# A state-space scan regrouped into turns over both channel halves of four sequences

## The reference

```
u = silu(conv(xin));  dt = softplus(...);  A = -exp(A_log)
def step(h, inp):                       # over 128 tokens
    dt_t, B_t, C_t, u_t = inp
    dA = exp(dt_t[..., None] * A)       # 256 channels x 16 states
    h = dA * h + (dt_t * u_t)[..., None] * B_t[:, None, :]
    y = einsum('bcn,bn->bc', h, C_t)    # sum over the 16 states
y = (y + u * D) * silu(z);  out = y @ wo.T
```

## Time and profile before

| | us |
|---|---|
| median of 3 runs | 2901.29 |
| profiled execution | 2900.32 |
| its span | 2898.6 |
| scan stage of layer 0, 1, 2 | 275.5, 259.5, 244.5 |
| DVE busy over the span | 1628.0 (56%) |
| PE busy | 2225.7 (77%) |
| POOL busy | 974.6 (34%) |

### The profile page before, as it was taken

The page is one execution under the profiler, slowest core; times in us unless marked ns, Lnnn a source line. Parts: engine busy times, 40 slices in busy tenths (PEclk is TensorE's granted clock), DMA queues, the critical chain, the costliest instruction groups (busy, mean ns, idle before and its releaser), DMA issues. The chain is left out here.

```text
span 2898.6 us, 39071 instructions
## 1 busy us (share of the span) xinstructions
PE 2225.7 (77%) x13654; PEld 1455.9 (50%) x13654; DVE 1628.0 (56%) x3279; ACT 1077.1 (37%) x2217; POOL 974.6 (34%) x926
## 2 busy tenths in 40 slices
PE   6999877999998668936539997569996388765691
PEld 4666544777787556934115555245553122244351
DVE  2333458656660141214259997689996799824352
ACT  2221112444443211412646663546663566401110
POOL 3001105445556013041015554045550366502104
PEclk7656567999999756977759999679998699956796
DMA  5000001111111003720000000000000000000462
GB/s 198 0 0 0 23 20 39 36 31 31 31 33 26 16 7 112 219 73 11 15 6 1 1 1 1 2 6 1 1 1 3 0 0 1 0 7 14 141 195 62
DMA packets 167830, 98.74 MB, mean 34 GB/s; under 512 B 89975, under 2 KB 151747, under 8 KB 166130
## 3 DMA queue, kind: packets, MB, share of 16 engines
q1 hardware_dynamic: 163058, 87.75, 10.9%
q0 software_dynamic: 4608, 8.86, 1.1%
HBM read 58.34 MB, written 38.80 MB: 34 GB/s over the span
## 5 line engine op out<-in xcount | busy, mean ns | idle before, releaser
L1255 POOL TENSOR_TENSOR mc_hc<-mc_states,mc_c_sb 128x1024 f32<-128x1024 f32 x192 | 452.8, 2358 | 327.6 <-DVE mc_states L1316 304.9
L1316 DVE TENSOR_TENSOR_SCAN mc_states<-psum,mc_dbu 128x1024 f32<-128x1024 f32 x192 | 439.8, 2290 | 14.6 <-issue 0.4
L1345 PE MATMUL psum<-mc_hc,ident 128*128 128x512 f32 x768 | 373.4, 609 | 6.5 <-POOL mc_hc L1255 6.5
L1277 ACT ACTIVATE mc_c_sb<-psum 128x512 f32<-128x512 f32 x384 | 225.7, 588 | 107.1 <-PE psum L1336 107.1
L1268 ACT ACTIVATE psum<-dt,a 128x1016 f32<-128x1016 f32 x192 | 213.5, 1112 | 110.9 <-DVE mc_states L1316 110.8
L1305 DVE TENSOR_TENSOR mc_dbu<-psum,dtu 128x1024 f32<-128x1024 f32 x192 | 233.5, 1216 | 9.9 <-PE psum L1328 9.0
L1345 PEld LDWEIGHTS psum<-mc_hc,ident 128*128 128x128 f32 x768 | 148.9, 195 | 126.5 <-issue 96.9
L594 POOL TENSOR_TENSOR fw_tmp<-zeros 128x30 f32<-128x30 f32 (+14 forms) x240 | 123.3, 514 | 256.4 <-DMA zeros<-fw_blocks 238.2
L1336 PE MATMUL psum<-bc,select 96*128 96x512 bf16 x384 | 152.6, 397 | 71.0 <-ACT mc_c_sb L1277 70.9
L1336 PEld LDWEIGHTS psum<-bc,select 96*128 96x128 bf16 x384 | 37.6, 98 | 272.1 <-ACT mc_c_sb L1277 254.2
L1670 POOL DMA_INDIRECT c_y<-slots_y,slots x64 | 64.0, 1000 | 306.0 <-PEq L1665 287.1
(11 more groups left out here) (379 smaller groups left out, 4455.8 us busy)
## 6 DMA issues: line engine op xcount, KB each, us to landing
e_w<-in_L_ffn_ew SPq DMA_DIRECT2D x64, 256.0 KB, 3.1
slots_x<-zeros SPq DMA_DIRECT2D x12, 1024.0 KB, 12.6
e_x<-slots_x SPq DMA_DIRECT2D x96, 128.0 KB, 2.3
slots_y<-e_y SPq DMA_DIRECT2D x96, 128.0 KB, 2.0
e_w<-in_L_ffn_w SPq DMA_DIRECT2D x64, 128.0 KB, 2.2
fw_blocks<-fw_A SPq DMA_DIRECT2D x128, 32.0 KB, 1.7
zeros<-fw_blocks SPq DMA_DIRECT2D x8, 512.0 KB, 3.4
fw_inverses<-fw_Y SPq DMA_DIRECT2D x8, 512.0 KB, 3.1
```

The source lines that it names most:

```text
L1255: nc.gpsimd.tensor_tensor(hc[:, k % 2, :], states[:, k % 2, :], c_sb[:, k % 2, :], ALU.mult).then_inc(s["hc_done"], 1)
L1277: nc.scalar.activation(c_sb[:, k % 2, j * 512:(j + 1) * 512], c_ps, ACT.Copy).then_inc(s["c_copied"], 1)
L1316: nc.vector.tensor_tensor_scan(out=states[:, k % 2, :], data0=decay_ps, data1=dbu[:, k % 2, :], initial=0.0, op0=ALU.mult, op1=ALU.add).th ...
L1345: last = nc.tensor.matmul(y_ps[:, j * 512:(j + 1) * 512], m.ident, hc[:, k % 2, j * 512:(j + 1) * 512], start=(n == 0), stop=(n == NSTATE ...
```

## The change

- A turn now covers both halves of four sequences (2 x 512 columns), so one B row and one C row serve both halves. There are still 64 turns per layer, in 4 chunks of 16, and two scans of 512 columns per turn.
- B: PE spreads the first `SPLIT` columns into `b_ps` (256 of 512 in layers 0 and 1, 320 in layer 2), which DVE multiplies for both halves. The other 256 (192) columns go to `rest_ps`, ACT copies them to `b_sb`, and POOL multiplies them two turns ahead (`rest`).
- C: the step-size stage copies the C rows to SBUF (ACT, four copies of 32x512) and writes them to DRAM; in the scan stage SP loads each row, broadcast to 128 partitions, up to four turns ahead.
- Accumulation: 8 matmuls of 32x32 weights (`eye`) per turn in place of 2 of 128x128. Half 1 goes from row group i to column group i+1; the weights of half 1 are permuted on the host to fit.
- u*D is 8 tile matmuls more at the start of each chunk (`skip_path`), and `finish` multiplies by the gate; the output stage loses its gating.
- LSTM: `whh` in two 64x64 quarters (8 matmuls for 4); the parts of the cell in one DVE instruction; the cell itself by two PE matmuls of 128x128 weights (`lstm_cell`), placed behind the accumulation of turn k-2 in PE's order.

The added lines of the scan, with what stands around them:

```diff
+    if f == 0:
+        for g in range(GROUPS):
+            act.wait_ge(s["split_done"], g + 1)
+            nc.scalar.activation(rows[DTR:2 * DTR, g, :], m.bank[g][DTR:2 * DTR, :], ACT.Copy).then_inc(s["rows_done"], 1)
...
+    CHUNKS = GROUPS
+    TURNS = CHUNKS * NSTATE
+    SPLIT = GT - (256 if lstm else 192)
...
+for k in range(TURNS):
+    c, cols, n = turn(k)
+    if k >= AHEAD:
+        sp.wait_ge(s["hc_done"], k - AHEAD + 1)
+    sp.dma_start(c_sb[:, k % AHEAD, :], c_rows[n:n + 1, cols].to_broadcast([P, GT])).then_inc(c_in[k % AHEAD], 16)
+    if k == NSTATE and layer < 2:
+        load_front(sp, io, m, z, layer + 1)
...
+def rest(k):
+    c, cols, n = turn(k)
+    pool.wait_ge(s["b_copied"], k + 1)
+    nc.gpsimd.tensor_tensor(dbu[:, k % 2, :, SPLIT:GT], z["dtu"][:, :, c * GT + SPLIT:(c + 1) * GT],
+                            b_sb[:, k % 2, :].unsqueeze(1).to_broadcast([P, HALVES, GT - SPLIT]), ALU.mult).then_inc(s["rest_done"], 1)
+rest(0)
+rest(1)
 for k in range(TURNS):
+    pool.wait_ge(s["scan_done"], 2 * k + 2)
+    pool.wait_ge(c_in[k % AHEAD], 16 * (k // AHEAD + 1))
     if k >= 2:
         pool.wait_ge(s["y_mm"], k - 1)
+    nc.gpsimd.tensor_tensor(hc[:, k % 2], states[:, k % 2], c_sb[:, k % AHEAD, :].unsqueeze(1).to_broadcast([P, HALVES, GT]),
+                            ALU.mult).then_inc(s["hc_done"], 1)
+    if k + 2 < TURNS:
+        rest(k + 2)
...
+def decay(k, f):
+    c, cols, n = turn(k)
+    if k >= 1:
+        act.wait_ge(s["scan_done"], 2 * (k - 1) + f + 1)
+    nc.scalar.activation(decay4[:, f, :, 1:P], z["dt"][:, f, cols].rearrange("p (b t) -> p b t", b=GS)[:, :, 1:P], ACT.Exp,
+                         scale=z["a"][:, f, n:n + 1]).then_inc(s["decay_done"], 1)
+def copy_b(k):
+    act.wait_ge(s["rest_mm"], k + 1)
+    if k >= 2:
+        act.wait_ge(s["rest_done"], k - 1)
+    nc.scalar.activation(b_sb[:, k % 2, :], rest_ps, ACT.Copy).then_inc(s["b_copied"], 1)
+nc.scalar.activation(decay4[:, :, :, 0:1].rearrange("p f b o -> p (f b) o"),
+                     z["dt"][:, 0, 0:HALVES * GS].unsqueeze(2), ACT.Copy, scale=0.0)
+if lstm:
+    nc.scalar.activation(cell_ps, r["cell"][:, :], ACT.Copy).then_inc(s["cell_set"], 1)
+copy_b(0)
+copy_b(1)
...
+    decay(k, 0)
     if lstm:
         act.wait_ge(s["step_mm"], k + 1)
+        nc.scalar.activation(gates[:, :], step_ps[:, 0:3 * BATCH], ACT.Tanh)
+        nc.scalar.activation(fresh_ps, step_ps[:, CELL * BATCH:(CELL + 1) * BATCH], ACT.Tanh).then_inc(s["gates_done"], 1)
+    decay(k, 1)
     if lstm:
+        act.wait_ge(s["cell_mm"], k + 1)
+        nc.scalar.activation(tanh_ps, cell_ps, ACT.Tanh, scale=0.5).then_inc(s["tanh_done"], 1)
+    if k + 2 < TURNS:
+        copy_b(k + 2)
...
+def finish(c):
+    dve.wait_ge(s["y_mm"], NSTATE * (c + 1))
+    cols = slice(c * GT, (c + 1) * GT)
+    nc.vector.tensor_tensor(z["y"][:, :, cols], y_ps, z["gate"][:, :, cols], ALU.mult).then_inc(s["y_done"], 1)
 for k in range(TURNS):
+    c, cols, n = turn(k)
+    dve.wait_ge(s["b_mm"], k + 1)
+    nc.vector.tensor_tensor(dbu[:, k % 2, :, 0:SPLIT], b_ps[k % 2][:, 0:SPLIT].unsqueeze(1).to_broadcast([P, HALVES, SPLIT]),
+                            z["dtu"][:, :, c * GT:c * GT + SPLIT], ALU.mult).then_inc(s["dbu_done"], 1)
+    if n == 2 and c > 0:
+        finish(c - 1)
     if lstm:
         dve.wait_ge(s["gates_done"], k + 1)
+        nc.vector.scalar_tensor_tensor(out=parts[:, :], in0=gates[:, BATCH:3 * BATCH], scalar=1.0, in1=fresh_cell_ps, op0=ALU.add,
+                                       op1=ALU.mult).then_inc(s["parts_done"], 1)
+    dve.wait_ge(s["dbu_done"], k + 1)
+    dve.wait_ge(s["rest_done"], k + 1)
     if k >= 2:
         dve.wait_ge(s["hc_done"], k - 1)
+    for f in range(HALVES):
+        dve.wait_ge(s["decay_done"], 2 * k + f + 1)
+        nc.vector.tensor_tensor_scan(out=states[:, k % 2, f, :], data0=decay_ps[:, f, :], data1=dbu[:, k % 2, f, :], initial=0.0,
+                                     op0=ALU.mult, op1=ALU.add).then_inc(s["scan_done"], 1)
+        if lstm and f == 0:
+            dve.wait_ge(s["tanh_done"], k + 1)
+            nc.vector.scalar_tensor_tensor(out=hs[:, first_step + k + 1, :], in0=gates[:, 0:BATCH], scalar=1.0, in1=tanh_ps,
+                                           op0=ALU.add, op1=ALU.mult).then_inc(s["hidden_done"], 1)
...
+def tiles(weights, src, f, start, stop):
+    for i in range(P // QUARTER):
+        rows = slice(QUARTER * i, QUARTER * (i + 1))
+        to = QUARTER * ((i + f) % (P // QUARTER))
+        last = nc.tensor.matmul(y_ps[to:to + QUARTER, f, :], weights[rows, :], src[rows, :], start=start, stop=stop,
+                                skip_group_check=True)
+    return last
+def skip_path(c):
+    if c > 0:
+        pe.wait_ge(s["y_done"], c)
+    else:
+        pe.wait_ge(s["diag_done"], 2)
+    for f in range(HALVES):
+        last = tiles(diag[:, f, :], z["u"][:, f, c * GT:(c + 1) * GT], f, True, False)
+    last.then_inc(s["du_mm"], 1)
 def accumulate(k):
+    c, cols, n = turn(k)
+    if n == 0:
+        skip_path(c)
     pe.wait_ge(s["hc_done"], k + 1)
+    for f in range(HALVES):
+        last = tiles(eye[:, :], hc[:, k % 2, f, :], f, False, n == NSTATE - 1)
     last.then_inc(s["y_mm"], 1)
...
+        for d in range(2):
+            rows = slice(HD * d, HD * (d + 1))
+            last = nc.tensor.matmul(step_ps[rows, q * BATCH:(q + 1) * BATCH], r["whh"][rows, q, rows], hs[rows, first_step + k, :],
+                                    start=False, stop=(q == GATES - 1), skip_group_check=True)
     last.then_inc(s["step_mm"], 1)
+def lstm_cell(k):
+    pe.wait_ge(s["parts_done"], k + 1)
+    nc.tensor.matmul(cell_ps, half_ident[:, :], parts[:, BATCH:2 * BATCH], start=True, stop=False, skip_group_check=True)
+    nc.tensor.matmul(cell_ps, m.ident, parts[:, 0:BATCH], start=False, stop=True, skip_group_check=True).then_inc(s["cell_mm"], 1)
+broadcast_rest(0)
+broadcast_b(0)
+broadcast_rest(1)
 for k in range(TURNS):
     if lstm:
         lstm_step(k)
     if k >= 2:
         accumulate(k - 2)
+    if lstm:
+        lstm_cell(k)
+    if k + 2 < TURNS:
+        broadcast_rest(k + 2)
+    if k + 1 < TURNS:
+        broadcast_b(k + 1)
```

More of the change, by code:

```diff
@@ L1127, in mamba_step_size_stage @@
         rest = sb("rest", [32, GROUPS, GT])
+        rows = sb("rows", [2 * DTR, GROUPS, GT])
         e, w = z["y"], z["dtu"]
@@ L1220, in sb @@
             return mem.enter_context(nc.sbuf_tensor("mc%d_%s" % (layer, name), shape, dt))
[L1221 to L1230, removed]
-        step_ps = step_bank[:, 0:GATES * BATCH]
[L1232 to L1236, removed]
+        dbu = sb("dbu", [P, 2, HALVES, GT])
+        states = sb("states", [P, 2, HALVES, GT])
+        hc = sb("hc", [P, 2, HALVES, GT])
+        c_sb = sb("c_sb", [P, AHEAD, GT])
+        b_sb = sb("b_sb", [P, 2, GT - SPLIT])
+        eye, diag = sb("eye", [P, QUARTER]), sb("diag", [P, HALVES, QUARTER])
+        c_in = [s["c_in%d" % i] for i in range(AHEAD)]
+        c_rows = io["c_rows"][layer]
+        half_ident = sb("half_ident", [P, P])
+        b_ps, step_bank = m.bank[0:2], m.bank[2]
+        decay_ps = m.psum[:, 4:6, :]
+        decay4 = decay_ps.rearrange("p f (b t) -> p f b t", b=GS)
+        y_ps = m.psum[:, 6:8, :]
+        step_ps = step_bank[:, 0:GATES * BATCH]
+        fresh_cell_ps = step_bank[:, 64:64 + 2 * BATCH]
+        fresh_ps, cell_ps = fresh_cell_ps[:, 0:BATCH], fresh_cell_ps[:, BATCH:]
+        tanh_ps = step_bank[:, 96:96 + BATCH]
+        rest_ps = m.bank[3][:, 0:GT - SPLIT]
+        bc = z["bc"]
+        hs, gates, parts = r["hs"], r["gates"], r["parts"]
         def turn(k):
-            return k // (HALVES * NSTATE), k // NSTATE % HALVES, k % NSTATE
+            c = k // NSTATE
+            return c, slice(c * GT, (c + 1) * GT), k % NSTATE
         with nc.Block() as block:
@@ L1321, in _ @@
+                finish(CHUNKS - 1)
+                dve.wait_ge(s["y_done"], CHUNKS)
             @block.tensor
```

125 lines of the change are left out of this document (37 added, 88 removed).

## The result

The changed kernel takes **2962.65 us** (median of 4 runs, 2949.12 to 2977.78), against 2898.43 for the kernel before beside it (4 runs, 2892.48 to 2923.44): a ratio of 1.0206, with a 95% interval of 1.012 to 1.0293. It is slower by about 64 us. The forecast was 2984, in a range of 2860 to 3022. The profiled execution, the shortest of the four, has a span of 2947.4, 48.8 over the 2898.6 of before. Now and then an execution takes some 50 to 110 us longer than the others of its kernel, at a lower mean granted clock; medians are of all runs, ratios and intervals leave such executions out.

The account below looks back on a forecast made before the run. DVE bounded the old turns; PE's LSTM chain at half clock would bound the new LSTM turns. 77 + 13 - 8 + 7 + 3 - 4 - 5 = +83 on 2900.3 gives 2984 us, range 2860 to 3022.

Parts of the forecast that it names:

- Which clock: PE in both LSTM scan stages: half clock for most of them, short returns at chunk boundaries; chance 0.57.
- clock stays up: Rival for the LSTM turns: PE keeps full clock, POOL bounds the turn at 3.73, total 2872; chance 0.23.
- Rival 3: Accumulation: tiles sharing rows take turns, 3.58 at half clock, 1.88 at full; chain 3.9 to 4.0, total 2905; chance 0.05.
- The half-clock turn: LSTM chain on PE: 1.45 + 1.79 + 0.85 + 0.5 = 4.6, 0.6 over the old turn, 128 x 0.6 = 77.
- The returns of the clock: Chunk boundaries of the LSTM stages: short returns to full clock give about 8 us back.
- POOL's turn: POOL's work per scan turn at 3.73 in LSTM layers, 3.46 in layer 2, ahead of DVE.
- Boundaries: Chunk starts: PE waits for `finish`, then does `skip_path`; 3.4 over a turn, 2.2 more than before, 13 in sum.
- Step size: Step-size stage: four copies of 32x512 at 0.59 stand ahead of the Ln DVE waits for; 2.4 x 3 = 7.
- C by DMA: Scan stage: one 256 KB load per turn, four ahead, landing in about 3.1 like `e_w`, costs nothing.
- Drains between tiling modes: Four tiling-mode changes per turn on PE: taken as nothing; 0.1 each would give 51 more, carrying the upper end.
- the start of `eye` and `diag`: Making eye and diag at the start: 1 x 3 us more.
- the gating: Output stage: its gating, 4.63 in four pieces before, is removed; -4 us.

Follow-up runs that it names:

- Experiments 1: Changed kernel with its accumulation into y and skip path as 128x128 matmuls instead of 32x32 tiles: 2879.28 us, ratio 0.9925 to the kernel before.
- experiment 3: Changed kernel with both channel halves on the same four diagonal 32x32 tiles, the second half no longer shifted: 2899.21 us, ratio 1.0006 to the kernel before.
- experiment 6: Kernel before the change with the two accumulation matmuls of a turn cut to 16 columns each instead of 512: 3056.24 us, one run.
- experiment 5: Changed kernel with one unread selection matmul of 512 columns in each turn of layers 0 and 1: 2952.55 us, one run.
- experiment 7: Changed kernel with ScalarE's copies of the C rows in the step-size stage moved behind both Lns: 2970.57 us, one run.
- experiment 2: Changed kernel with two unread selection matmuls of 512 columns from 96 rows in each turn of layers 0 and 1: 2920.19 us, ratio 1.0074.
- the second version: Changed kernel with two unread matmuls a turn, more at boundaries, thirty ending the step-size stage, six in the first turn, late C copies: 2880.71 us, ratio 0.9933.
- Experiment 8: Changed kernel with two unread matmuls of 512 columns from 32 rows in each turn of layers 0 and 1: 2943.34 us, one run.

## Why the prediction was right, step by step

- **Which clock: right, and the step that decides.** 0.59 was measured over each of the two LSTM layers, 0.50 inside their slow turns, as forecast. Experiments 1, 3 and 6 show that the cause is how much the accumulation streams: with 1.98 or 1.92 at full clock the clock is up, with 1.09 it is mostly not, with almost none never. The rival "clock stays up" is dead for this kernel. Its 2872 is near the 2879 of wide matmuls by chance: that version's turn of 3.74 contains an accumulation twice as long as the rival's. Rival 3's premise was tested in experiment 3; its 2905 against 2899.
- **The half-clock turn: mis-sized, 4.6 against 4.97.** Of the four terms the step took 1.64 from the hidden state to the accumulation's start (I had 1.45), the accumulation 1.89 (1.79), the cell 0.87 (0.85), the tail 0.57 (0.5): 4.97 together. The largest miss is the pre-gate matmul, 0.62, which I had left at 0.4 within the 1.45. The term was 128 x 0.6 = +77; 76 turns at 4.97 made +74. That PE's own sum "is as long" as the chain of 4.6 holds for the 4.6 (4.56 by experiment 5) and not for the chain, which is 0.4 longer.
- **The returns of the clock: mis-sized the other way.** I took 8 us. There were 32 turns at about 3.5, 48 us less than at 4.97. The sum of the 126 intervals came to +69, where my terms gave 77 + 13 - 8 = +82 for these layers. The short half-clock turn (0.37 x 76 = 28 us) and the missing returns (40 us) largely cancel; that is luck.
- **POOL's turn: 3.73 against 3.54.** The 0.08 between two instructions, put in twice, was too much: records of 2.34 and 1.27 follow one another at 2.31 and 1.24 from start to start, 3.55 in all. Layer 2 is 3.27, not 3.46, and gave 17.7 us where I had 5.
- **Boundaries: close.** At half clock throughout, 5.58 + 7.34 is 2.98 over two turns; I had 3.4. The other five boundaries are shorter, since the clock rose in them. The wait for `finish` is 1.19 there.
- **Step size: right in kind, 2.05 against 2.4 a layer** (experiment 7).
- **C by DMA: right.** `mc_c_sb<-c_rows` lands in 3.1 us, as `e_w` does, and no `hc` waited for it.
- **Drains between tiling modes: not shown apart.** The turn is 0.37 over my 4.6, of which the pre-gate matmul explains 0.22. The accumulation, between two such changes, took 1.89 from start to start where I had 1.79; whatever a drain costs is inside such differences, so the 0.4 a turn that carried my upper end did not come in full.

The median came out 21 us under the forecast. The profiled execution shows more, since it is 13.5 us under the median: its span grew by 48.8 where the sum had +83. Of that the LSTM layers have 13 (+69 for +82), layer 2 has 13 (-17.7 for -5), and the rest of the span 8 (-2.3 for +6). In that rest the copies are the 6 that I expected; the start of `eye` and `diag` and the gating were not measured apart, and the stretch ahead of the first scan alone differs between the traces by up to 29 us (1513.0 to 1542.0).

About the fall of the clock the Trainium skill, "TensorE: Matmul & The Clock Gate", section "HAM oscillation — how this bites in real kernels", speaks of PE's idle gaps. The traces agree in part: the losses of experiment 2 and of the second version came at pauses of 1.84 and 1.76. But in the changed kernel the clock also fell inside chunks, where PE's longest pause was 0.74. The Trainium skill, on the same page, section "What's actually happening", says that activity releases the throttle. Busy time alone did not, with records over 59.57 of 60.00 us here, 272.27 of 280.00 in experiment 6, and 241.27 of 243.00 in experiment 2.

**Open.** What a matmul has to be to count is not settled: columns, rows or work per time. Experiment 8 speaks against rows for keeping the clock and says nothing on getting it back. Why one of two like boundaries lost the clock isn't known, nor why some chunk starts bring it up and others, with the same work, don't.

## What to carry to other kernels

Before taking work off TensorE, look at which records bring its clock up; if the time goes to short matmuls behind them, halving them can cost more than it gives (1.88 to 1.09 us of accumulation, and the turn from 4.00 to 4.97). Read PEclk beside PE busy: where PE has hardly a pause at 0.50 and the other engines wait for it, more streaming may be the cure. Do not take "busy" for the bound, though: ends are modelled, and here 0.4 us of a turn of 4.97 went into a wait. Here a burst of unread matmuls helped where dense work followed it and the later pauses were filled; put ahead of pauses it was lost. Compare stretches and not only totals: of the 150 us in experiment 6, 66 were the two LSTM layers'.

## What the runs showed of the hardware

- TensorE busy 272.27 of 280.00 us with matmuls of 16 and 64 columns and four row copies of 512 columns a turn ran at 0.50 throughout (experiment 6); cutting its work made the LSTM turns 4.59 in place of 4.00.
- Two matmuls a turn from 32 rows kept the clock at 1.00 over 218 us; with none, in the changed kernel, it was lost after 4 to 9 turns.
- The clock has memory: in one run the same program text ran layer 0 at 3.54 a turn and layer 1, from its first boundary on, at 5.42 (experiment 2).
- 32x32 tiles that share rows and not columns run side by side (1.09 for 16 records of 512 columns); with both halves on the same tiles they take turns (1.92).
- A 2 KB row spread over 128 partitions by DMA lands as fast as the 256 KB load `e_w`, 3.1 us.
- GpSimd's products follow one another without a pause: 2.34 and 1.27 us in 3.55 from start to start.
